# Post-norm transformer layer on eight cores: value projection spread into attention, second LayerNorm moved into the last expert step, first weight loads issued later

## The reference

```
q, k, v = x @ w_q + b_q, x @ w_k + b_k, x @ w_v + b_v          # 16 heads of 64
out  = softmax(q . k[window of 7] / 8, out-of-sequence masked) @ v[window of 7]
x    = layernorm(x + out @ w_o + b_o)
comb = softmax over the two largest of (x @ gate_w + gate_b), 0 elsewhere
y    = sum over e of comb[:, e] * (relu(x @ w1[e] + b1[e]) @ w2[e] + b2[e])
x    = layernorm(x + y)
```

## Time and profile before

| | us |
|---|---|
| median of 3 runs (lowest, highest) | 5052.81 (5049.91, 5056.19) |
| time of the profiled execution | 5051.68 |
| its span on the slowest core (first to last instruction) | 5050.1 |
| spans of the eight cores | 5043.4 to 5050.1 |
| TensorE busy | 4314.7 |
| ScalarE, VectorE busy | 1172.4, 1088.6 |

### The profile page before, as it was taken

The page is one execution under the profiler, slowest core; times in us unless marked ns, Lnnn a source line. Parts: engine busy times, 40 slices in busy tenths (PEclk is TensorE's granted clock), DMA queues, the critical chain, the costliest instruction groups (busy, mean ns, idle before and its releaser), DMA issues. The chain is left out here.

```text
span 5050.1 us, 53567 instructions; the slowest of 8 cores (5043.4 to 5050.1 us)
## 1 busy us (share of the span) xinstructions
PE 4314.7 (85%) x19624; PEld 1916.2 (38%) x19624; DVE 1088.6 (22%) x2736; ACT 1172.4 (23%) x2460; POOL 146.7 (3%) x176
## 2 busy tenths in 40 slices
PE   5644489999999999999876444999999999999996
PEld 2221234444444444444332222344444444444443
DVE  0233311122112211222202333122211221122112
ACT  3323322111221122112243223211122112211222
POOL 0000000000000000000000000000000000000000
PEclk9755579999999999999986555899999999999998
DMA  5100034444444344444530000444444444443442
GB/s 86 17 9 13 5 56 78 71 79 68 83 67 84 67 81 70 79 72 75 97 71 5 9 11 3 67 75 75 72 79 71 80 67 84 67 84 67 80 71 67
DMA packets 149770, 310.94 MB, mean 62 GB/s; under 512 B 3641, under 2 KB 4025, under 8 KB 149453
## 3 DMA queue, kind: packets, MB, share of 16 engines
q0 software_dynamic: 144096, 289.49, 34.6%
q1 hardware_dynamic: 5422, 18.03, 1.0%
HBM read 588.60 MB, written 8.39 MB: 118 GB/s over the span
## 5 line engine op out<-in xcount | busy, mean ns | idle before, releaser
L871 PE MATMUL m_pY<-m_w2b,m_hg 128*128 128x512 bf16 x8192 | 1778.3, 379 | 72.6 <-ACT m_hg L848 72.6
L831 PE MATMUL m_pH<-s_xt,m_w1b 128*128 128x512 bf16 x8192 | 1782.0, 380 | 0.0
L848 ACT ACTIVATE m_hg<-m_pH,s_b1pc 128x512 bf16<-128x512 f32 x1024 | 703.5, 687 | 2861.6 <-PE m_pH L831 2861.6
L886 DVE SCALAR_TENSOR_TENSOR m_acc<-m_pY,s_comb,m_acc 128x512 f32<-128x512 f32 x1024 | 721.8, 747 | 2983.8 <-PE m_pY L871 2983.8
L871 PEld LDWEIGHTS m_pY<-m_w2b,m_hg 128*128 128x128 bf16 x8192 | 796.8, 98 | 1054.1 <-issue 102.4
L831 PEld LDWEIGHTS m_pH<-s_xt,m_w1b 128*128 128x128 bf16 x8192 | 802.3, 98 | 971.6 <-issue 7.6
L458 PE MATMUL h_pj<-h_v_tm,h_attnT 128*128 128x64 bf16 x256 | 54.1, 211 | 281.6 <-DVE s_rSt L428 184.5
L396 DVE SCALAR_TENSOR_TENSOR h_smx<-h_pj,s_consts,s_masks 128x134 f32<-128x134 f32 x256 | 90.1, 352 | 440.8 <-PE h_pj L386 440.6
L458 PEld LDWEIGHTS h_pj<-h_v_tm,h_attnT 128*128 128x128 bf16 x256 | 26.7, 104 | 322.0 <-issue 322.0
L633 PE MATMUL h_ptb<-s_id_bf,h_o_sb 128*128 128x128 bf16 x128 | 26.9, 271 | 125.7 <-POOL h_o_sb L620 108.8
L474 ACT ACTIVATE h_o_sb<-h_pj,s_rSt 128x64 bf16<-128x64 f32 x256 | 80.2, 313 | 221.2 <-PE h_pj L466 219.7
(11 more groups left out here) (84 smaller groups left out, 1186.4 us busy)
## 6 DMA issues: line engine op xcount, KB each, us to landing
m_w1b<-w POOLq DMA_DIRECT2D x64, 2048.0 KB, 15.4
m_w2b<-w POOLq DMA_DIRECT2D x64, 2048.0 KB, 15.6
h_x_own<-xh SPq DMA_DIRECT2D x16, 512.0 KB, 3.8
out<-s_ostg SPq DMA_DIRECT2D x16, 512.0 KB, 2.7
s_xb<-xh POOLq DMA_DIRECT2D x16, 256.0 KB, 4.1
s_wbuf<-wq POOLq DMA_DIRECT2D x2, 2048.0 KB, 26.9
s_wbuf<-wk POOLq DMA_DIRECT2D x2, 2048.0 KB, 37.6
s_wbuf<-wv POOLq DMA_DIRECT2D x2, 2048.0 KB, 16.9
```

The source lines that it names most:

```text
L831: e.matmul(pH[jj % 2][:, 0:512], w1b[0][:, ic * GCOLS + j * 128: ic * GCOLS + j * 128 + 128], xt1[:, ic * HALF_T + ts * 512: ic * HALF_T + ...
L848: e.activation(hg[:, j * HALF_T + ts * 512: j * HALF_T + ts * 512 + 512], pH[jj % 2][:, 0:512], AF.Relu, bias=b1pc[:, e_i * 32 + g_i * 8 + ...
L871: e.matmul(pY[t % 2][fs][:, 0:512], hg[:, j * HALF_T + t * 128: j * HALF_T + t * 128 + 128], w2b[0][:, j * GCOLS + fs * 512: j * GCOLS + f ...
L886: e.scalar_tensor_tensor(acc[:, t * D + fs * 512: t * D + fs * 512 + 512], pY[t % 2][fs][:, 0:512], comb[:, t * 8 + e_i: t * 8 + e_i + 1], ...
```

## The change

Four things are changed.

1. `emit_prefetch` gets an argument, and at the start of half 0 it loads only the two x tiles. wq and wk of half 0 are issued by POOL at the end of A1, behind the last x tile. Half 1 is as before.
2. In A2 the value projection makes tiles 0 to 4 only. Tiles 5 to 8 are made by a new function `vdrip` in A3, after the output projection of token tiles 2, 3, 4 and 5, into the two PSUM banks that the scores use (`pj[0]`, `pj[1]`). Scores wait for the eviction of what was there, and the product with v waits for its tile of v.
3. The negative mean of both LayerNorms is made on DVE (a multiplication by a constant -1/1024 from `consts`) and no longer on ACT.
4. LN2 becomes a function `emit_l2(t)`, called for tile t in step 31 right behind the tile's additions to `acc`.

```diff
-        emit_prefetch(0)
+        emit_prefetch(0, weights=False)
...
+                    wq_ev = p.op("pool", lambda e: e.dma_start(
+                        wbuf[0][:].rearrange("p (c n) -> p c n", c=8),
+                        wq_d.ap().rearrange("(c p) n -> p c n", p=128)), inc="sWQ0", k=16)
...
                 p.flush("A1_h%d" % half)
...
-                for vt in range(9):
-                    rows = 128 if vt < 8 else 6
+                for vt in range(5):
...
+                def vdrip(vt, guards):
+                    rows = 128 if vt < 8 else 6
+                    ev = None
+                    for fs in range(2):
+                        last = None
+                        for ic in range(8):
+                            last = p.op(
+                                "pe",
+                                lambda e, ic=ic, vt=vt, rows=rows, fs=fs:
+                                e.matmul(pj[fs][0:rows, 0:512],
...
+                                waits=(guards + [wv_ev]) if ic == 0 else (), inc=None)
...
+                        ev = p.op("act",
+                                  lambda e, vt=vt, rows=rows, fs=fs:
+                                  e.copy(v_tm[0:rows, vt * D + fs * 512: vt * D + fs * 512 + 512],
+                                         pj[fs][0:rows, 0:512]),
+                                  waits=[last], inc="sACT")
+                        vchain_bank[fs] = ev
+                    vrdy[vt] = ev
...
+                    if 2 <= t <= 5:
+                        vdrip(t + 3, [sm_ev[(t0_, 15)], sm_ev[(t1_, 15)]])
...
-                    nm_ev = p.op("act",
-                                 lambda e, sp8=sp8: e.mul(scr[:, sp8 + 3:sp8 + 4],
-                                                          scr[:, sp8 + 2:sp8 + 3], -1.0 / D),
-                                 waits=[s1_ev], inc="sACT")
+                    nm_ev = p.op("dve",
+                                 lambda e, sp8=sp8:
+                                 e.tensor_single_scalar(scr[:, sp8 + 3:sp8 + 4],
+                                                        scr[:, sp8 + 2:sp8 + 3],
+                                                        consts[:, 3:4], AluOpType.mult),
+                                 waits=[s1_ev], inc="sDVE")
...
+                            if step == 31:
+                                emit_l2(t)
```

More of the change, by code:

```diff
@@ L180, in emit_prefetch @@
                     inc="sXB%d" % (t % 2), k=16)
+            if not weights:
+                return
             pre[(h, "wq")] = p.op("pool", lambda e: e.dma_start(
@@ L259, in build_nc @@
                         emit_xld(t + 2)
-                wq_ev = pre[(half, "wq")]
-                wk_ev = pre[(half, "wk")]
+                if (half, "wq") in pre:
+                    wq_ev = pre[(half, "wq")]
+                    wk_ev = pre[(half, "wk")]
+                else:
+                    wq_ev = p.op("pool", lambda e: e.dma_start(
+                        wbuf[0][:].rearrange("p (c n) -> p c n", c=8),
+                        wq_d.ap().rearrange("(c p) n -> p c n", p=128)), inc="sWQ0", k=16)
+                    wk_ev = p.op("pool", lambda e: e.dma_start(
+                        wbuf[1][:].rearrange("p (c n) -> p c n", c=8),
+                        wk_d.ap().rearrange("(c p) n -> p c n", p=128)), inc="sWQ1", k=16)
                 p.flush("A1_h%d" % half)
@@ L325, in build_nc @@
                                 "pe",
[L326 to L328 removed]
+                                lambda e, ic=ic, bank=bank, vt=vt, fs=fs:
+                                e.matmul(pj[bank][0:128, 0:512],
+                                         xt_ext[:, ic * EXT + vt * 128: ic * EXT + vt * 128 + 128],
                                          wbuf[0][:, ic * D + fs * 512: ic * D + fs * 512 + 512],
@@ L333, in build_nc @@
                             "pe",
-                            lambda e, bank=bank, rows=rows, fs=fs:
-                            e.matmul(pj[bank][0:rows, 0:512], ones64(rows),
+                            lambda e, bank=bank, fs=fs:
+                            e.matmul(pj[bank][0:128, 0:512], ones64(128),
                                      bnd[64:65, fs * 512: fs * 512 + 512],
@@ L339, in build_nc @@
                         ev = p.op("act",
-                                  lambda e, bank=bank, vt=vt, rows=rows, fs=fs:
-                                  e.copy(v_tm[0:rows, vt * D + fs * 512: vt * D + fs * 512 + 512],
-                                         pj[bank][0:rows, 0:512]),
+                                  lambda e, bank=bank, vt=vt, fs=fs:
+                                  e.copy(v_tm[0:128, vt * D + fs * 512: vt * D + fs * 512 + 512],
+                                         pj[bank][0:128, 0:512]),
                                   waits=[last], inc="sACT")
                         pj_ev[bank] = ev
+                vrdy = {}
+                vchain_bank = [None, None]
+                def vdrip(vt, guards):
[8 more added lines that the diff above has]
+                                e.matmul(pj[fs][0:rows, 0:512],
+                                         xt_ext[:, ic * EXT + vt * 128: ic * EXT + vt * 128 + rows],
+                                         wbuf[0][:, ic * D + fs * 512: ic * D + fs * 512 + 512],
+                                         start=(ic == 0), stop=False),
+                                waits=(guards + [wv_ev]) if ic == 0 else (), inc=None)
+                        last = p.op(
+                            "pe",
+                            lambda e, rows=rows, fs=fs:
+                            e.matmul(pj[fs][0:rows, 0:512], ones64(rows),
+                                     bnd[64:65, fs * 512: fs * 512 + 512],
+                                     start=False, stop=True),
+                            waits=(), inc="sPE")
+                        ev = p.op("act",
[5 more added lines that the diff above has]
+                    vrdy[vt] = ev
                 p.flush("A2_h%d" % half)
```

128 lines of the change are left out of this document (66 added, 62 removed).

## The result

The changed kernel takes 5004.69 us (median of 8 runs) where the kernel before takes 5054.62 beside it: a ratio of 0.9901, 95% interval 0.9889 to 0.9914. It is faster, by about 50 us, and outside the predicted range (4961 to 4996): a third of the predicted 75.5 is missing.

What follows compares the result with a forecast made beforehand. TensorE was taken as the longest engine, with time to gain only at the seams between its work. Terms 7.3 + 13.2 + 55.3 - 0.3 = 75.5 us gave 4977 us; range 4961 to 4996.

Steps and rivals of the forecast that it cites:

- first loads: A1 of half 0: third x tile's wait falls, TensorE then waits for wq, q starts 7.3 us earlier; bounds 1.9 to 19.0.
- value tiles out of A2: A2: four value tiles of two groups, 2.88 us a group, leave each half: 46.1 us gained in all.
- square held back in A3, with the mean's move: A3: evictions ahead of the LayerNorm's square delay it 4.1 us at eight places, 32.9 us; the mean's move loses 0.3.
- output projections: A3: the sixteen rise to 2.4 GHz earlier or later, reshuffled by any shift; put at 10 us either way.
- LN2: Last expert step: LN2 beside TensorE's work, VectorE at 3.66 us a tile, gains 27.65 us a half, 55.3 in all.
- The mark that was named for it: Start of half 0: the prediction is wrong if q starts later than 72.71.
- TensorE does not feel it: Last expert step: VectorE falls back 0.21 us a tile, 1.45 at the eighth, without making TensorE wait.
- A low clock at the new matmuls: Rival, A3: new value groups run at 1.2 GHz; 5019 us if all eight places, 4998 if half; chance 8%.
- A2 of half 0 run at 1.2 GHz: Slower case: after 12 us of TensorE idle the clock stays low through A2, adding 88 us, 5065; chance 2%.
- VectorE, or the stores, set the pace of the last step: Rival, last expert step: 4.16 us a tile, 7 us less gained, 4984; about 4990 with late stores; chance 10%.

Runs made afterwards that it cites:

- the eight more matmuls: The kernel before, with eight matmuls of the last value group made once more at the end of A2 in each half, result unused: ratio 1.0008.
- the first loads alone: The kernel before, with only wq and wk of half 0 issued at the end of A1: median 5059.2 us, ratio 1.0020.

## Why the prediction was right and wrong

The terms beside what the stages show (after, cores 0 to 3, less the kernel before, all cores), in us:

| term | predicted | measured |
|---|---|---|
| first loads (A1, half 0) | -7.3 | +4.5 |
| value tiles out of A2 | -46.1 | -45.7 |
| square held back in A3, with the mean's move | +33.2 | +34.0 |
| output projections | 0 (up to 10 either way) | +3.1 |
| rest of A3, A1 of half 1 | 0 | +1.9 |
| LN2 | -55.3 | -51.2 |
| sum | -75.5 | -53.4 |

*First loads: the step that failed.* The prediction said that TensorE waits for wq and that "wk lands one such load later (82 at most) and is wanted half-way through the 59.08 us of q and k, at about 95; that work hides it". Its durations were good: wq predicted to land 16.9 us after its issue, measured 15.9, and the issue at 43.48 was even earlier than the 48.4 reckoned. But q also stands behind a barrier, the barrier waits for POOL's DMAs, and wk was one of them. The slack was counted at the reader of wk, where there was plenty, and not at the barrier, where there was none. "DMAs may run across a barrier", as the description of the kernel before has it, is not so for POOL's: in this kernel, and in the four others that load wq at the end of A1, the next stage starts 1.0 to 1.4 us after POOL's last load has landed. Whether the barrier itself or POOL's own queue does the waiting, no run separates. The experiment with wk behind the barrier gives 12.7 us in A1 and puts A1 8.2 us below the kernel before; predicted were 7.3. With that move alone the kernel takes 4987 us, inside the predicted range; of the 22.1 us between the two sums, 11.8 are this term. The mark that was named for it, q starting later than 72.71, is met: 73.34.

The trace of before had the hint, and it was overlooked. POOL's timeline of the setup, kernel before, core 7:

```profile
2.26 0.57 POOL L159 DMA_DIRECT2D s_gwb<-gw_r  x1
11.44 1.07 POOL L179 DMA_DIRECT2D s_xb<-xh  x2 [8.61 <-DVEq L57]
```

Its DMA row for that load:

```profile
s_gwb<-gw_r POOLq DMA_DIRECT2D x1, 16.0 KB, 8.4
```

In a stage in which no engine computes, POOL stood 8.61 us at the barrier, until 0.8 us after its own small load had landed (2.26 + 8.4 = 10.7).

*Value tiles: right, with their price.* What leaves A2, what a place costs (3.8 to 4.03 us for 4.1) and why are as worked out, and the experiment with the evictions moved gives the price back whole (32.8 us on the mean core for the 32.9 of the prediction). Some 1.3 us of the 34.0 are the three new groups at 1.2 GHz, 1.8 us each over four cores. What was missed is that this price is no property of the move: the same copies, written behind the scaling, cost nothing.

*Output projections.* Their sums moved by +6.4 and -3.3 us, within the 10 allowed. A shift alone moved those of half 1 by 9.0, so it takes no cost of the value tiles to explain this; that there is none is not shown. But the spread is wider: over the timed runs the slowest core lies 12.5 us above the mean of the cores, before 6.3, while the mean core gained 56.5. Since the time is that of the slowest core, about 6 us of the shortfall are that; that the output projections make this spread fits the stages (on cores 0 to 3 A3 of half 0 runs from 485.0 to 496.3 us, their sums from 62.4 to 71.6) and the eight more matmuls, where a shift alone took it from 7.4 to 12.7.

*LN2: the right mechanism, a term too small.* VectorE's tile was put at 3.66 us and takes 3.91. The mean is 0.32 to the centring where 0.34 was reckoned; the 0.25 more lie between the additions and the residual sum: 2508.25 - 2506.66 = 1.59 where 1.33 was taken from the earlier trace rows. There the sum read tile 0, whose additions were long over; now it reads what the addition just ahead of it writes. Timeline of the second tile, after core 0:

```profile
2487.17 1.41 DVE L995 SCALAR_TENSOR_TENSOR m_acc<-m_pY,s_comb,m_acc 128x512 f32<-128x512 f32 x2
...
2488.68 1.23 DVE L835 SCALAR_TENSOR_TENSOR s_r<-s_x1f,m_acc 128x1024 f32<-128x1024 f32 x1
```

These are 1.51 us. From the third tile on it is 1.59, and there the sum also waits for ScalarE's scaling of the tile before the last; that this second wait makes the further 0.08 is likely, and not shown. Seven tiles fall 0.25 us further behind each, 1.75 a half, 3.5 in all of the 4.1 missing. With VectorE at 3.91 a tile against TensorE's 3.45 the fall back is 3.2 us at the eighth tile, and TensorE does wait, 0.16 us; "TensorE does not feel it" was wrong by that.

A rule bears on this. The Trainium skill, "VectorE: DVE Perf Modes", section "The DRAIN you can't avoid", says of eight copies that a semaphore between consecutive VectorE operations costs nothing extra (13.88 us with one after each and with one after the last alone). In this trace an operation that waits for the one just ahead of it and reads its result does come later: 1.51 us for 1.33. If the rule held for such operations too, LN2 would have gained the 55.3 that were predicted. The prediction's estimate of 0.06 us for the mean, from the same page, is not borne out: its row, core 0:

```profile
L843 DVE TENSOR_SCALAR s_scr<-s_scr,s_consts 128x1 f32<-128x1 f32 x16 | 3.4, 214 | 1.7
```

*The rivals.* A low clock at the new matmuls came at 3 of 64 groups only, 1.8 us each; nor did A2 of half 0 run at 1.2 GHz: its 24 us of idle TensorE ahead left q and k at 59.31 us, as in the earlier trace rows. The time falls where the first of these put it (4998 to 5019 us), for other reasons. "VectorE, or the stores, set the pace of the last step" came halfway: the pace is 3.91 us, between the 3.66 of the forecast and its 4.16, and the late store cost nothing.

*The range.* The bounds that the prediction names beside its forecast (5.4 us for the first loads, 7.1 for LN2, 10 for the output projections) add up to 5000 above 4977, not to its 4990 or 4996; the measured time lies above that as well.

## What to carry to other kernels

Before a transfer is moved, look for what else waits for it than its reader: the queue, the barrier that closes the stage it is now in, and the engines behind that barrier. Where work is put into another engine's gap, follow the small operations that it brings along; here eight gaps held the matmuls, and the evictions, written ahead of the square, cost 33 us. A chain repacked so that an operation reads what the one just ahead of it wrote can be longer than the sum of its operations' spacings measured elsewhere, here by 0.25 us a tile.

## What the runs showed of the hardware

- The barrier that closes a stage opens only after POOL's DMAs have landed, whether or not the next instructions need them: q starts 1.0 to 1.4 us after wk in the changed kernel and with the first loads alone, and as long after wq with wk moved. SP's are not waited for: its eight stores of half 0 are issued until 2518.19, the next stage starts at 2518.79, and a store takes 2.6 us. SyncE's row, after core 0:

```profile
2490.78 27.41 SPq L882 DMA_DIRECT2D out<-s_ostg  x8
```

- VectorE starts a sum that needs the additions just ahead of it 0.18 us later than one that does not (1.51 us after their start for 1.33), and 0.26 later where it also waits for ScalarE (1.59).
- An output projection begins at 1.2 GHz and rises to 2.4 in its first group (7.9 us in all at most), in its second (up to 10.3) or not before its end (10.7 to 11.1: 3 of 128 in the kernel before, 6 of 64 on cores 0 to 3 of the changed one). Some 2.2 us more work at the end of A2 moved the mean sum of half 1's eight by 9 us, and of half 0's by 2.6. What decides it is open.
